# A ninth field on TensorE, GpSimd resting after every eight gathers, three row buffers

## The reference, cut to what matters

```python
sp_emb = emb_tables[fidx, sp_input]                 # 2048 x 26 x 32: one row of each field's table
lin_vals = lin_tables[fidx, sp_input, 0]
lin_output = ds_input @ lin_w.T + lin_b + jnp.sum(lin_vals, axis=1, keepdims=True)
s = jnp.sum(sp_emb, axis=1)
bi_pooled = 0.5 * (s * s - jnp.sum(sp_emb * sp_emb, axis=1))
x = jnp.concatenate([bi_pooled, ds_input], axis=1)  # 45 wide
h = jax.nn.relu(x @ w1.T + b1)                      # 256
h = jax.nn.relu(h @ w2.T + b2)                      # 128
out = jax.nn.sigmoid(h @ fw.T + fb + lin_output)
```

## Time and profile before

| what | value |
|---|---|
| three timed runs, median (lowest to highest) | 466.59 us (463.79 to 466.76) |
| the profiled execution, its own time | 468.15 us |
| span of the profiled execution, first to last instruction | 466.4 us |
| what lies around the span | 1.75 us |
| mean granted clock of TensorE in the span | 0.951 |
| PE / DVE / ACT / POOL busy, share of the span | 88% / 71% / 55% / 61% |

### The profile page before, as it was taken

One profiled execution on the slowest core, in us unless ns is written; L12 is line 12 of the kernel. 1 busy time (PEld: TensorE's weight loads), 2 busy tenths in 40 slices (PEclk: granted clock), 3 DMA queues, 4 the chain that ended last, 5 costly groups with the idle time before them and its releaser, 6 DMA issues.

```text
span 466.4 us, 5488 instructions
## 1 busy us (share of the span) xinstructions
PE 410.4 (88%) x1797; PEld 337.5 (72%) x1798; DVE 332.0 (71%) x358; ACT 258.5 (55%) x450; POOL 284.2 (61%) x309
## 2 busy tenths in 40 slices
PE   8999799799789779789799979979979759979977
PEld 5788578688678668678688858768868645647735
DVE  8869569669649749559739849567787678677733
ACT  6799836356645644744564654665376358542133
POOL 6657557557557547566566657557557557566740
PEclk9999899899899999899899988998999997999959
DMA  7611141111511104111050112411142101001100
GB/s 207 189 29 27 21 164 26 21 21 17 172 13 27 22 10 166 21 25 23 10 179 11 24 23 36 153 23 12 24 145 38 12 11 13 10 12 12 15 9 0
DMA packets 17124, 23.02 MB, mean 49 GB/s; under 512 B 6245, under 2 KB 16183, under 8 KB 16186
## 3 DMA queue, kind: packets, MB, share of 16 engines
q1 hardware_dynamic: 7560, 17.62, 11.7%
q0 software_dynamic: 9536, 5.05, 10.0%
HBM read 22.61 MB, written 0.04 MB: 49 GB/s over the span
## 4 chain that ended last, share of the span: by engine, by line
PE 29%; DVE 24%; another core or an unknown queue 20%; issue 17%; ACT 7%; DMA 1%; SPq 0%; DVEq 0%; ACTq 0%
PE cand L899 12%; PE cand L902 12%; DVE masked L492 8%; DVE gates L467 7%; DVE low L479 4%; DVE picks L552 2%; ACT gates L726 2%; DVE pick_sq L555 2%; ACT distance L718 2%; PE cand L946 1%; DMA stage<-tabs 1%; ACT high L693 1%; PE bank_b L921 1%; PE cand L956 1%
## 5 line engine op out<-in xcount | busy, mean ns | idle before, releaser
L373 POOL DMA_INDIRECT rows<-table,row_idx x293 | 278.3, 950 | 162.5 <-issue 75.8
L899 PE MATMUL cand<-high,gates 128*128 128x462 f32 x826 | 319.6, 387 | 20.9 <-issue 19.5
L902 PE MATMUL cand<-low,gates 128*128 128x462 f32 x826 | 317.5, 384 | 19.2 <-issue 19.1
L899 PEld LDWEIGHTS cand<-high,gates 128*128 128x128 f32 x826 | 161.5, 196 | 53.0 <-issue 32.7
L902 PEld LDWEIGHTS cand<-low,gates 128*128 128x128 f32 x826 | 161.0, 195 | 45.8 <-issue 27.7
L492 DVE TENSOR_TENSOR masked<-cand,mask 128x924 f32<-128x924 f32 x58 | 64.8, 1117 | 92.5 <-remote 89.1
L500 DVE TENSOR_REDUCE picks<-masked 128x66 f32<-128x924 f32 x56 | 106.8, 1908 | 1.9
L726 ACT ACTIVATE gates<-distance,one 128x512 fp32r<-128x512 bf16 (+1 forms) x128 | 83.7, 703 | 10.9 <-remote 10.9
L718 ACT ACTIVATE distance<-codes,minus_key 128x512 bf16<-128x512 f16 (+1 forms) x119 | 77.8, 704 | 0.1
L706 ACT COPY bank_b<-high 128x462 f32<-128x462 f32 x47 | 25.8, 549 | 92.3 <-issue 61.3
L467 DVE TENSOR_SCALAR gates<-bank_a,key_of 128x512 fp32r<-128x512 f32 (+1 forms) x82 | 56.1, 736 | 1.1 <-issue 1.1
(11 more groups left out here) (114 smaller groups left out, 124.2 us busy)
## 6 DMA issues: line engine op xcount, KB each, us to landing
stage<-tabs SPq DMA_DIRECT2D x7, 1617.0 KB
rows<-table,row_idx POOLq DMA_INDIRECT x293
codes<-codes_dram SPq DMA_DIRECT2D x27, 128.0 KB
stage<-tabs SPq DMA_DIRECT2D x7, 231.0 KB, 2.9
idx_raw<-sparse SPq DMA_DIRECT2D x1, 208.0 KB
w_sb<-w2t SPq DMA_DIRECT2D x1, 128.0 KB
dense_sb<-dense_cols SPq DMA_DIRECT2D x1, 120.0 KB
x_and_y<-dense_rows SPq DMA_DIRECT2D x1, 112.0 KB
```

What stands on the lines that cost most here:

```text
L373: pool.indirect_dma_start(out=to, out_offset=None, in_=table[:, :], in_offset=bass.IndirectOffsetOnAxis(ap=row_idx[:, at:at + 1], axis=0), ...
L899: first = nc.tensor.matmul(to, gate, high[f % 2][:, k, :], start=(k == 0), stop=False)
L902: last = nc.tensor.matmul(to, gate, low[f % 2][:, k, :], start=False, stop=(k == CHUNKS - 1))
```

## The change

MMF becomes 9. Fields 0 to 7 are matched for all tiles (32 jobs) and the ninth for tiles 8 to 11 and the last two, so there are 34 jobs with 134 pairs of a field and a tile. GF is 18 for ten tiles and 17 for six: 282 gathers. RING becomes 3. TensorE's increments of `half_tile_begun` and POOL's waits on them are gone. In their place POOL waits, before gathers 8, 16, 24 and so on, until the gather before has landed (`landed_at`); this stops inside the last tile's end part, so there are 34 such waits. TILE_AT sums tiles at jobs 2, 4, 6, 9, 11, 13, 15, 18, 20, 22, 24 and 27. To make room in SBUF, `idx_wrap` and a part of `idle` go, and the arrays of `find_codes` are folded from 128 to 72 partitions and from 128 to 256 columns.

```diff
-    RING = 4
+    RING = 3
...
-    TILE_AT = {2 * t + 2: t for t in range(TILES - 5)}
+    TILE_AT = {2 * t + 2 + (t + 1) // 4: t for t in range(TILES - 5)}
...
-    HALVES = (0, 4)
-    AHEAD = 400
-    LET_OF = [[30, 30, 30, 440, 40, 40, 40, 340]] + [[135, 101] * TB] * (NJ - 5) + [[175] * 8, [175] * 8, [150] * 8, [280] * 4]
...
-    def begun_until(n):
-        return min(h for h in range(len(LET)) if AHEAD + LET[h] > 100 * n)
-
+    REST = 8
+
+    def landed_at(n):
+
+        t = max(u for u in range(TILES) if sum(GF[:u]) <= n)
+        return t % RING, 16 * (n + 1 - sum(GF[u] for u in range(t) if u % RING != t % RING))
...
-        idx_wrap = sb("idx_wrap", [P, TILES * F], i32)
...
-        col_raw = sb("col_raw", [R, P], i32)
-        col_wrap = sb("col_wrap", [R, P], i32)
-        col_hi = sb("col_hi", [R, P], i32)
-        col_code = sb("col_code", [R, P], fp16)
+        col_raw = sb("col_raw", [R // 2, 2 * P], i32)
+        col_wrap = sb("col_wrap", [R // 2, 2 * P], i32)
+        col_hi = sb("col_hi", [R // 2, 2 * P], i32)
+        col_code = sb("col_code", [R // 2, 2 * P], fp16)
...
-            sp.dma_start(codes_dram, col_code[:, :]).then_inc(codes_out, 16)
+            sp.dma_start(codes_dram.rearrange("(r k) p -> r (k p)", k=2), col_code[:, :]).then_inc(codes_out, 16)
...
-                    if begun_until(n) > 0 and begun_until(n) > begun_until(n - 1):
-                        pool.wait_ge(half_tile_begun, begun_until(n))
+                    if n > 0 and n % REST == 0 and not (t == LAST and g > SPLIT):
+
+                        slot, count = landed_at(n - 1)
+                        pool.wait_ge(gathered[slot], count)
                         pool.nop(nofuse=True)
...
-                nc.vector.tensor_scalar(idx_wrap[:, :], idx_raw[:, :], 0, CATS, ALU.is_lt, ALU.mult).then_inc(idx_step, 1)
+                wrap = masked[1][:, :, :].rearrange("p t m -> p (t m)")[:, 0:TILES * F]
+                nc.vector.tensor_scalar(wrap, idx_raw[:, :], 0, CATS, ALU.is_lt, ALU.mult).then_inc(idx_step, 1)
...
-                first = nc.tensor.matmul(to, gate, high[f % 2][:, k, :], start=(k == 0), stop=False)
-                if k in HALVES:
-                    first.then_inc(half_tile_begun, 1)
+                nc.tensor.matmul(to, gate, high[f % 2][:, k, :], start=(k == 0), stop=False)
...
-                    nc.tensor.matmul(spare, idle[:, 0:P], idle[:, :], start=True, stop=True)
+                    nc.tensor.matmul(spare, idle[:, :], idle[:, 0:1].broadcast_to([P, N]), start=True, stop=True)
...
-    P, M = 128, 8
+    P, M = 128, 9
```

More of the change, by code:

```diff
@@ L131, in build_deep_fm @@
     AT_A = {(2, 3): TURN, (2, 6): L1A, (3, 1): L1B, (3, 4): L2}
-    HALVES = (0, 4)
-    AHEAD = 400
-    LET_OF = [[30, 30, 30, 440, 40, 40, 40, 340]] + [[135, 101] * TB] * (NJ - 5) + [[175] * 8, [175] * 8, [150] * 8, [280] * 4]
-    LET = [0] + list(itertools.accumulate(itertools.chain.from_iterable(LET_OF)))
-    assert len(LET) == 1 + sum(SIZE) * len(HALVES)
-    assert AHEAD + LET[-1] > 100 * sum(GF)
-    def begun_until(n):
-        return min(h for h in range(len(LET)) if AHEAD + LET[h] > 100 * n)
+    REST = 8
+    def landed_at(n):
+        t = max(u for u in range(TILES) if sum(GF[:u]) <= n)
+        return t % RING, 16 * (n + 1 - sum(GF[u] for u in range(t) if u % RING != t % RING))
     COLS = [slice(g[0] % TB * P, g[-1] % TB * P + P) for g in GROUPS]
@@ L190, in build_deep_fm @@
         one = sb("one", [P, 1])
-        idle = sb("idle", [P, N], bf16)
+        idle = sb("idle", [P, P], bf16)
         stage = sb("stage", [P, TW])
@@ L267, in build_deep_fm @@
         act_gates = sem("act_gates")
-        half_tile_begun = sem("half_tile_begun")
         half_matched = sem("half_matched")
@@ L401, in other_rows @@
             def other_rows():
-                nc.vector.tensor_scalar(idx_wrap[:, :], idx_raw[:, :], 0, CATS, ALU.is_lt, ALU.mult).then_inc(idx_step, 1)
+                wrap = masked[1][:, :, :].rearrange("p t m -> p (t m)")[:, 0:TILES * F]
+                nc.vector.tensor_scalar(wrap, idx_raw[:, :], 0, CATS, ALU.is_lt, ALU.mult).then_inc(idx_step, 1)
                 dve.wait_ge(idx_step, 1)
-                nc.vector.scalar_tensor_tensor(idx_wrap[:, :], idx_raw[:, :], last_row[:, 0:1], idx_wrap[:, :], ALU.min,
+                nc.vector.scalar_tensor_tensor(idx_raw[:, :], idx_raw[:, :], last_row[:, 0:1], wrap, ALU.min,
                                                ALU.add).then_inc(idx_step, 1)
@@ L408, in other_rows @@
                 nc.vector.scalar_tensor_tensor(
-                    row_idx[:, F:].rearrange("p (t f) -> p t f", f=F), idx_wrap[:, F:].rearrange("p (t f) -> p t f", f=F),
+                    row_idx[:, F:].rearrange("p (t f) -> p t f", f=F), idx_raw[:, F:].rearrange("p (t f) -> p t f", f=F),
                     0, field_base[:, :].unsqueeze(1).broadcast_to([P, TILES - 1, F]), ALU.max, ALU.add).then_inc(idx_set, 1)
@@ L435, in find_subs @@
                 nc.vector.tensor_scalar(sub_hi[:, :].rearrange("p (t f) -> p t f", f=MMF),
-                                        idx_wrap[:, :].rearrange("p (t f) -> p t f", f=F)[:, :, 0:MMF], 0, CATS - 1,
+                                        idx_raw[:, :].rearrange("p (t f) -> p t f", f=F)[:, :, 0:MMF], 0, CATS - 1,
                                         ALU.max, ALU.min).then_inc(sub_step, 1)
@@ L1125 @@
         "sparse": np.ascontiguousarray(sp.reshape(B // P, P, F).transpose(1, 0, 2)).reshape(P, (B // P) * F),
-        "cols": np.ascontiguousarray(sp[:, :M].T).reshape(M * (B // P), P),
+        "cols": np.ascontiguousarray(sp[:, :M].T).reshape(M * (B // P) // 2, 2 * P),
         "table": np.concatenate([both, np.repeat(both[:, -1:, :], 97 * (P - 1), axis=1)], axis=1).reshape(-1, E + 1),
```

## The result

The changed kernel takes 463.87 us (median of 20 executions, 455.3 to 467.34), the kernel before in the same set 465.57 us (20 executions, 461.87 to 470.17). The medians differ by 1.7 us, 0.4%. The ratio compares only executions within 1.5% of the fastest of each kernel, 8 of 20 of the changed one and 18 of 20 of the kernel before, and is 0.9865 [0.9826, 0.9904]. The profiled execution took 463.93 us, with a span of 462.2 us. So the ninth field is paid for, and what is left is 0.4% by the medians and a little over 1% among the quicker executions, too little to call a gain; forecast were 451 us and a span of 450.4.

A forecast was written before the change was run, and what follows sets the result against it. Bound: POOL's sequencer sticks after some ten gathers and holds up TensorE's increments, on top of PE's stream. Span 466.4 - 10 - 9 + 2 + 1 = 450.4 us, 452.2 with 1.75 around it, so 451 against the median; range 440 to 500.

The forecast's parts named there:

- What bounds the kernel: Whole kernel: after some ten gathers POOL's sequencer sticks, TensorE's increments don't arrive; 44 us of PE pauses in the middle.
- The pace on `half_tile_begun` doesn't prevent it: Kernel before: POOL's waits on TensorE's increments don't stop the sticking of POOL's sequencer; no size of its own.
- (1) Ninth field: PE's stream: 134 pairs of field and tile in place of 118, 47.0 us more, all on the path.
- (2) The rests: POOL's queue: 34 waits for a landing, 1.65 us each over the pitch, 56 us (43 to 85), last gather at 415.
- rests dearer, 3.8 us: POOL's queue: each rest takes 3.8 us, last gather at 443, 462 to 470 us, no difference; chance 0.08.
- (3) What the freeze gives back: PE's pauses and late increments go: middle (45 to 365 us) -10 us, last stretch (365 to 457 us) -9 us.
- (4) What is late next: DVE fits with 1.3 us slack per job, POOL just keeps level with the tiles wanted; 2 us added for slips.
- (5): Small edits (RING 3, `find_codes`, `idle`, `wrap`, dropped increments) cost nothing or nearly; 1 us for `find_codes` in job 0.
- The freeze stays: Rival: PE's pauses go on with each gather despite the rests, 44 us more in the middle, 513 us; chance 0.14.
- The instruction fetch: Rival: PE's pauses are its own instruction fetch and grow with its instructions, 64 us, time 523 us; chance 0.02.
- Holes without freeze: Rival: POOL's holes of 2.83 us stay besides the rests, POOL gets late, last gather at 480, 497 us; chance 0.13.
- the signs listed: PE: 95 matmuls per 20 us, "issue" gaps below 8 us; DVE "remote" below 20; last gather 400 to 443; clock 0.98.

The follow-up runs named there:

- small tables: Changed kernel, rests of eight, loads of the tables of fields 1 to 8 cut to the first of seven chunks (results left wrong): 442.77 us, ratio 1.1424.
- second set: Kernel before, changed kernel, changed kernel without rests and with a sliding window, run together: 459.32 (460.08 as the set's reference), 461.01, 614.47 and 609.91 us.

## Why the prediction was wrong, and what of it held

**What bounds the kernel.** Right in the main, wrong about POOL. DVE's masks do come late because TensorE's increments do, by 6.6 us in the median of the masks that DVE idled for in the kernel before against 0.04 us where nothing disturbs; this goes with POOL's gathers, and standing often keeps it small: "remote" fell to 15.3 us. Wrong is "its sequencer sticks until they are through": the kernel without rests shows POOL issuing on while PE crawls. In the kernel before, POOL's holes are its own waits on `half_tile_begun`, for increments that are late like DVE's. The gather at 102.26 needs the 52nd, of a matmul that PE began at 95.26, 4 us before the hole; for every hole between 45 and 365 us PE had begun the matmul 3.9 to 9.1 us before. I read it so: back-to-back gathers hold up the increments, POOL runs out of them and stands, and then they come. "The pace on `half_tile_begun` doesn't prevent it" is true of the late increments, but the pace limits the loss: 460 to 466 us, where nine fields with neither pace nor rest take 614. That run has no increments of `half_tile_begun` and crawls most, so the crawl doesn't need these; TensorE's other increments are in every kernel.

**(1) Ninth field**, 47.0 us: measured 47.4, with the small edits in it, where nothing else disturbs.

**(2) The rests: this is the term that failed.** A rest was put at 1.65 us over the pitch, 56 us in all, last gather at 415. Measured: 99.2 us of rests less 34 x 0.30 of ordinary gaps is 89 us, and the last gather at 449. Of the 33 us too few, 34 x 0.27 = 9 us are the plain rest: it leaves 2.2 us, so 1.9 over the pitch, more than the landing alone but well inside the bounds of 1.25 to 2.5. (The bound from above is no rest, but a wait for a late increment, and the earlier trace rows has a larger one without a pause of PE, 2.90 us; it changes nothing.) The other 24 us are eleven long rests, 19 of them the six beside table loads. The rows that the bounds came from held none of them: both the hole of 2.83 us in the earlier trace rows lie where no table load is under way, and beside 1.6 MB of table a rest takes up to 5.6 us more. With an average rest of 2.9 us of idling, 3.9 from issue to issue, the case that came is the rival "rests dearer, 3.8 us", which gave the last gather at 443 and 462 to 470 us, and had a chance of 0.08; it priced every rest alike, where 23 cheap and eleven dear ones make up the same sum. The prediction also had an estimate from the Trainium skill (DMA: Bandwidth & Descriptors, "Anatomy of one DMA — SWDGE (gpsimd) path"), a rest of 0.75 us over the pitch. That is less than half of the 1.9 us measured here for a plain rest.

**(3) What the freeze gives back.** The middle and the edits around it: forecast -10 + 2 + 1 = -7 us, measured -4 (19 matmuls ahead), with 5.5 us of the difference spent at 292 us, where DVE waited for a tile. The last stretch: forecast -9, measured 0. The waits of DVE and ACT for "remote" fell there from 25.6 to 9.1 us, but PE's wait of 12.0 us at 417 us, behind ACT's wait for the gathers of a tile, took their place; and the end follows the last gather by 13 us.

**(4) What is late next.** Named right ("POOL keeps level and no more"), priced too low: 2 us for slips, where the two stalls alone are 17.5 us. The forecast itself had said that POOL's lateness decides "from about 1 us more per rest on"; the average was 1 us more (89 / 34 = 2.6 for 1.65).

**(5)** The edits at nothing: the first 45 us are 9 matmuls better, not worse, so the 1 us for `find_codes` wasn't needed. That RING = 3 costs nothing can be seen from POOL never waiting for `reduced` beside its rests.

**The rivals.** "The freeze stays" is out for rests of eight as far as PE's pauses go; increments are still 2.9 us late there. The instruction fetch is out: PE has 224 matmuls more and its "issue" gaps are gone. "Holes without freeze" is out. Of the signs listed, those of the freeze came (14 of the 18 stretches of 20 us from 20 to 380 us have 95 matmuls or more), and those of POOL didn't: last gather at 449, eleven gaps beyond 2.4 us, clock 0.974 and not 0.98.

**What stays open.** By what path gathers hold up TensorE's increments, and whether the crawl comes from increments piling up. The debt is a rule fitted to rests of ten to twelve that then gave the time with nine, and missed several of its places; which resource it counts, no view shows. Nor does any show why the same program on the same chip crawls in one set and not in another. The changed kernel wasn't run in a set where before takes 388 us; since a rest every ten takes 438.8 to 439.2 there and small tables 442.8, it would hardly be under these: some 13% slower than before or more, an inference and no measurement.

## What to carry to other kernels

Price a wait for a DMA's landing where the queue is full, not only where it is empty: look for the same wait beside the largest transfer of the kernel, and take the mean over all places. When one engine pauses and another shows holes, don't decide from one trace which stands for which; take the suspected brake off, and measure from the end of an instruction to the start of the one that it releases, in a trace with the disturbance and in one without. And before a change is built against a disturbance, find out whether the disturbance is always there: here the answer to "is it faster?" is 0 to 1% faster, or probably 13% slower, by the kind of set.

## What the runs showed of the hardware

- TensorE's matmul stream slowed to starts 0.70, 1.40, 2.1 or 2.8 us apart (0.21 usual) beside gathers by GpSimd issued every 1.25 us, from about the 12th without a stand on (from the 20th in the first run of gathers), and recovered 1.5 to 3.5 us into a stand, once 7.5; its granted clock was 0.50 from 40 to 80 us of that run (nine fields without rests, second set).
- A DVE instruction waiting for a TensorE increment started 0.04 us behind the matmul's end in the sets without the disturbance. Beside the gathers in the others it was 2.9 us (changed kernel), 6.6 us (kernel before) and 10.7 us (no rests) in the median, though TensorE ran at full pace when it made many of them.
- The same kernel took 388 us in two sets and 459 to 466 us in four, two chips having been in both kinds; one without rests took 435 and 614 us on one chip.
- Rests after every 8, 9, 10, 11 and 12 gathers gave 461 to 464, 482, 526, 538 and 552 us in sets with the disturbance, and 435 to 439 us for ten to twelve in sets without it.
- A wait for the landing of the last of eight gathers left GpSimd 2.2 us idle, and up to 7.8 us where a 1.6 MB load was in the queues.
